# Local attention's scores three half tiles ahead of the turning, the first three behind the last feed-forward chunks

## The reference

```python
def _layer(x, wqkv, qs, ksc, wo, lg, lb, w1, b1, w2, b2):
    h = shift_token(x)
    q, k, v = jnp.split(h @ wqkv, 3, axis=-1)          # 8 heads of 64
    q = l2norm(q) * qs
    k = l2norm(k) * ksc
    q, k = rotary_xpos(q, k)
    o = local_attention(q, k, v)                       # window 128, looks one window back
    x = x + o @ wo
    h = layernorm(shift_token(x)) * lg + lb
    a, g = jnp.split(h @ w1 + b1, 2, axis=-1)          # hidden 682
    return x + (a * gelu(g)) @ w2 + b2
```

## Time and profile before

| what | value |
|---|---|
| median of 3 runs | 3101.23 us (3095.96 to 3109.24) |
| time of the profiled execution | 3108.76 us |
| its span | 3107.0 us |
| PE busy (matmul) | 2775.4 us, 89% of the span |
| DVE busy | 1622.3 us, 52% |
| ACT busy | 1200.9 us, 39% |
| POOL busy | 1076.6 us, 35% |

### The profile page before, as it was taken

One profiled execution on the slowest core, in us unless ns is written; L12 is line 12 of the kernel. 1 busy time (PEld: TensorE's weight loads), 2 busy tenths in 40 slices (PEclk: granted clock), 3 DMA queues, 4 the chain that ended last, 5 costly groups with the idle time before them and its releaser, 6 DMA issues. The chain is left out here.

```text
span 3107.0 us, 42331 instructions
## 1 busy us (share of the span) xinstructions
PE 2775.4 (89%) x15646; PEld 1867.6 (60%) x15646; DVE 1622.3 (52%) x3890; ACT 1200.9 (39%) x2254; POOL 1076.6 (35%) x769
## 2 busy tenths in 40 slices
PE   6999999999999999899989898999988579999990
PEld 3565656656565655645454545465544378999990
DVE  6656566565655555676767676767654310000002
ACT  4444453534444354444444444444442212222221
POOL 5423333342323333354535353535332201111112
PEclk9999999999999999999999999999987689999995
DMA  3000000000001011001010101010101179998875
GB/s 131 11 23 16 27 25 25 14 25 22 17 25 56 24 42 47 14 4 48 4 49 4 49 4 48 4 48 4 41 4 41 36 299 341 351 343 327 325 283 165
DMA packets 86054, 261.73 MB, mean 84 GB/s; under 512 B 10940, under 2 KB 50188, under 8 KB 67164
## 3 DMA queue, kind: packets, MB, share of 16 engines
q1 hardware_dynamic: 79372, 241.26, 21.4%
q0 software_dynamic: 6480, 17.77, 1.5%
HBM read 210.69 MB, written 44.12 MB: 82 GB/s over the span
## 5 line engine op out<-in xcount | busy, mean ns | idle before, releaser
L1176 POOL TENSOR_TENSOR s_qk<-s_qk,s_rrec 128x1024 f32<-128x1024 f32 (+1 forms) x128 | 215.7, 1685 | 578.4 <-DVE s_rrec L1330 578.2
L969 ACT ACTIVATE s_qk<-s_qk,s_mx 128x256 f32<-128x256 f32 (+1 forms) x512 | 239.9, 469 | 341.0 <-DVE s_mx L1324 340.3
L556 PE MATMUL s_pA<-s_w_wqkv,s_curT 128*128 128x512 f32 x768 | 354.7, 602 | 5.6 <-ACT s_curT L945 3.7
L1928 DVE COPY m_xT<-m_px 128x256 f32<-128x256 f32 x71 | 30.1, 425 | 475.5 <-PE m_px L1847 475.5
L1858 PEld LDWEIGHTS m_ph<-m_xT,m_w 128*128 128x128 f32 x2272 | 266.7, 193 | 5.4 <-issue 1.8
L1858 PE MATMUL m_ph<-m_xT,m_w 128*128 128x128 f32 x2272 | 267.3, 276 | 1.2 <-DVE m_xT L1928 1.2
L1872 PE MATMUL m_py<-m_w,m_hT 128*128 128x256 f32 x1136 | 256.8, 379 | 0.0
L556 PEld LDWEIGHTS s_pA<-s_w_wqkv,s_curT 128*128 128x128 f32 x768 | 142.6, 191 | 176.9 <-issue 163.4
L1419 DVE TENSOR_SCALAR s_pairs<-s_pD 128x1024 f32<-128x1024 f32 (+1 forms) x192 | 193.9, 1037 | 80.9 <-PE s_pD L699 79.3
L1792 POOL DMA_INDIRECT acc_s<-m_y,m_goal x71 | 68.1, 959 | 479.9 <-ACT m_y L1891 479.9
L1872 PEld LDWEIGHTS m_py<-m_w,m_hT 128*128 128x128 f32 x1136 | 210.4, 190 | 25.7
(11 more groups left out here) (224 smaller groups left out, 5172.5 us busy)
## 6 DMA issues: line engine op xcount, KB each, us to landing
m_w<-in_m_w SPq DMA_DIRECT2D x142, 1024.0 KB, 5.2
m_xin<-rows_s SPq DMA_DIRECT2D x71, 129.0 KB
m_acc<-acc_s SPq DMA_DIRECT2D x16, 512.0 KB, 5.2
s_cur<-in_x SPq DMA_DIRECT2D x8, 512.0 KB, 3.4
xn_s<-s_cur SPq DMA_DIRECT2D x8, 512.0 KB, 2.9
s_s_tm<-xn_s SPq DMA_DIRECT2D x8, 512.0 KB, 3.2
cur_s<-s_cur SPq DMA_DIRECT2D x8, 512.0 KB, 2.6
s_s<-s_s_tm SPq DMA_DIRECT2D x8, 512.0 KB, 2.6
```

Of the source, the lines that this page charges most:

```text
L556: last = nc.tensor.matmul(out, lhs(c), rhs(c), start=(c == 0), stop=(c == n - 1))
L969: last = nc.scalar.activation(pi, pi, ACT.Exp, scale=-1.0, bias=mx[:, u, i:i + 1], accum_out=rsum[:, u, i:i + 1])
L1176: nc.gpsimd.tensor_tensor(pi, pi, rrec[:, u, :].unsqueeze(2).broadcast_to((P, 4, 256 - lo)), ALU.mult).then_inc(p_rdy, 1)
```

## The change

`S` of half tiles 0, 1 and 2 moves from the u loop into the chunk loop, behind chunks 3, 4 and 5; `S` of half tile u + 1 then stands at u, from u = 2 on, behind `PT` of u - 2. DVE's `local_max`, ACT's `local_exp` and POOL's scaling move with it: `local_exp` of half tiles 0 and 1 stands behind the heads' copy of chunk 4 and behind the Gelu of chunk 5, that of half tile 2 at u = 1. In the u loop `PT` now stands ahead of `S` and of the latent scores' third round; on ACT `local_turned` stands ahead of `local_exp`. POOL scales half tiles 0 and 1 before and behind the second scatter of a latent stage.

```diff
             if s.ahead and c == 4:
                 j += [("qkT", k + 1, 3)]
+            if s.ahead and c >= NHC - 3:
+                j += [("S", k + 1, c - NHC + 3)]
         for u in range(2 * NT + 3):
-            if s.ahead and u < 2 * NT:
-                j += [("S", k + 1, u)]
             if s.ahead and 2 <= u < 2 * NT + 2:
                 j += [("PT", k + 1, u - 2)]
+            if s.ahead and 2 <= u < 2 * NT - 1:
+                j += [("S", k + 1, u + 1)]
...
                         heads_in(k + 1, 3)
+                    if s.ahead and c >= 4:
+                        local_exp(k + 1, c - 4)
                 for u in range(2 * NT + 3):
-                    if s.ahead and u < 2 * NT:
-                        local_exp(k + 1, u)
+                    if s.ahead and u == 1:
+                        local_exp(k + 1, 2)
                     if s.ahead and 2 <= u < 2 * NT + 2:
                         local_turned(k + 1, u - 2)
+                    if s.ahead and 2 <= u < 2 * NT - 1:
+                        local_exp(k + 1, u + 1)
...
+                if s.ahead:
+                    scale_probabilities(k + 1, 0)
+                if s.behind:
+                    scatter_rows(b - 1, 1)
+                if s.ahead:
+                    scale_probabilities(k + 1, 1)
...
                     if s.prep and c == 4:
                         again_apply(k + 1)
+                    if s.ahead and c >= NHC - 3:
+                        local_max(k + 1, c - NHC + 3)
+                    if s.ahead and c >= 4:
+                        local_reciprocal(k + 1, c - 4)
                     if s.behind and c == 5:
                         row_ends(b - 1, 1)
...
                 for u in range(2 * NT + 3):
-                    if s.ahead and u < 2 * NT:
-                        local_max(k + 1, u)
-                    if s.ahead and 1 <= u < 2 * NT + 1:
-                        local_reciprocal(k + 1, u - 1)
+                    if s.ahead and 2 <= u < 2 * NT:
+                        local_reciprocal(k + 1, u)
                     if s.lat and 6 < u < 11:
                         clipped(b, u - 7, (2,))
+                    if s.ahead and 2 <= u < 2 * NT - 1:
+                        local_max(k + 1, u + 1)
```

More of the change, by code:

```diff
@@ L870, in _ @@
                         head_transposes(k + 1, 3)
+                    if s.ahead and c >= NHC - 3:
+                        local_scores(k + 1, c - NHC + 3)
                 for u in range(2 * NT + 3):
-                    if s.ahead and u < 2 * NT:
-                        local_scores(k + 1, u)
+                    if s.ahead and 2 <= u < 2 * NT + 2:
+                        local_transposes(k + 1, u - 2)
                     if s.lat and 6 < u < 11:
                         latent_scores(b, u - 7, (2,))
-                    if s.ahead and 2 <= u < 2 * NT + 2:
-                        local_transposes(k + 1, u - 2)
+                    if s.ahead and 2 <= u < 2 * NT - 1:
+                        local_scores(k + 1, u + 1)
                     if s.ahead and u >= 3:
@@ L1226, in _ @@
                     scatter_rows(b - 1, 0)
-                    scatter_rows(b - 1, 1)
                 if s.prep:
                     reciprocal_roots(var_2, rstd_2, k + 1)
+                if s.ahead:
[4 more added lines that the diff above has]
+                    scale_probabilities(k + 1, 1)
                 if k == ITEMS - 1:
@@ L1235, in _ @@
                 for u in range(2 * NT + 3):
+                    if s.ahead and 2 <= u < 2 * NT:
+                        scale_probabilities(k + 1, u)
                     if s.ret and u in (4, 6, 8):
@@ L1243, in _ @@
                         query_sum(b, (u - 4) // 2)
-                    if s.ahead and u < 2 * NT:
-                        scale_probabilities(k + 1, u)
                     if s.lat and b == 0 and u == 2:
```

## The result

The changed kernel takes 3140.8 us (median of 4 runs) where the kernel before takes 3103.8 (median of 4): ratio 1.0124, 95% interval 1.0098 to 1.0151, 1.24% slower. That is above the range of 3090 to 3132. The profiled execution of the changed kernel takes 3139.22 us (span 3137.5), 30.5 more than the one of before; my sum had +6.

The account below looks back on a forecast made before the run. PE, busy 89% of the span, was taken as the bound. Retention -5.9, latent +10.2, stage -1 -5 and clock +7 gave +6 us, 3107 us on the median; range 3090 to 3132.

Parts of the forecast that it names:

- Chunk loop: Retention stages, up to w2: w2 starts 3.76 us later, 1.06 of it S2 done ahead, a loss of 2.70.
- the waits 0.73 and 0.72: Chunk loop, chunks 4 and 5: g waits for the banks of a heads' tile just turned, 0.73 and 0.72 us.
- w2's 1.77: End of the chunk loop: PE waits 1.77 us ahead of w2, behind the late Gelu and DVE's last fill.
- u loop of a retention stage: From w2 on: waits gone against new ones, stage end 627.6 instead of 628.14, -0.6 us a stage.
- The 2.83: Retention u loop: S4 waits 2.83 us in one piece for zaT's copy, which stands behind Exp 3 on ACT.
- Stage -1: Stage -1: no added load, the 3.20 ahead of S2 goes and five rounds gain 0.4 each, -5 us.
- Latent stages: Latent stages: w2 loses 2.2, net +1.4 us in six stages, +1.8 in stage 8, together +10.2.
- The clock: Whole program: waits of 2.83 and 4.0 bring more clock drops, 7 us taken, between nothing and 48.
- the second rival: Long waits bring the clock down in nearly every stage, 3 us for each of 14 stages: 3133 us, chance 0.2.
- the forecast: The prediction's own likeliest case, a near balance: +6 us, 3107 us on the median, chance 0.57.
- The tables: Chunk loop, before w2: a load is 1.28 us; two added loads cost 2.6 us and the Exp between 1.55.
- the third rival: A table switch costs about twice its load, w2 2.6 us later still in 15 stages: 3145 us, chance 0.03.

Follow-up runs that it names:

- exps_behind_gelu: The changed kernel with Exp of half tiles 0 and 1 behind the last Gelu on ScalarE, so no table loads are added: 3124.3 us, ratio 1.0061.
- scores_earlier: The changed kernel, early Exps behind the last Gelu, zaT and x1T emptied ahead of Exp, retention S0 and S1 behind chunks 1 and 2: 3061.8 us, 0.9865.
- stats_later: scores_earlier with the input statistics and norm of item k + 2 later on DVE in retention stages 0 to 5: 3064.3 us, ratio 0.9859.
- zat_first: The changed kernel with the emptying of zaT ahead of Exp 3 and of x1T ahead of Exp 5 on ScalarE: 3081.1 us, ratio 0.9925.
- first_three_only: The changed kernel with S of half tiles 0 to 2 still behind the chunks, but the u loop order of before: 3213.3 us, ratio 1.0334.
- the eight kernels named above: All kernels with the lead in the u loop and the statistics at u = 6; the product took 2.26 or 2.27 us in stages 0 to 5.

## Why the prediction was wrong

- **Chunk loop.** Right. Walked +3.76 to w2, measured +4.00; the waits 0.73 and 0.72 were 0.46 each, w2's 1.77 was 1.73. exps_behind_gelu and scores_earlier show both causes.
- **u loop of a retention stage.** This is the step that failed: "The sum: 580.77 + 42.8 + 2.83 + 1.2", -0.6 a stage. The 2.83 was there (2.69), but on the way from w2 to the next first product a clean stage takes 61.17, not 59.0. I had carried forward PE's work, the waits for ScalarE and one wait for DVE, and put the other waits for DVE at nothing. The clean stage of exps_behind_gelu has 5.9 us of waits (2.69, 0.78, 0.23, 1.08, 1.09) where I had 4.0. The 1.08 comes from a meeting that the lead brought about: DVE's product of the gated output runs beside POOL's scaling of a half tile and takes 1.58 longer. stats_later, where they don't meet, shows 1.16 of the 2.2. The 0.78 and the 0.23 (copies of outputs on DVE that TensorE now waits for; before, one such wait of 0.34) are read from the timeline only, and about 0.3 stay unassigned. A clean stage is 1.85 longer than before, seven of them 13 us, where I had -4.2.
- **Stage -1.** -5 was -0.5 (first product of stage 0 at 94.69, before 95.21). I left out that `zaT` is turned there too: S of half tile 4 waits 3.25 us. With the emptying first (zat_first), the first product of stage 0 comes at 92.58.
- **Latent stages.** Right in the sum: +1.4 a stage walked, and 72.66 + 85.35 - 156.83 = +1.2 without falls of the clock. The waits walked at 4.0, 0.73 and 1.02 are 3.5, 0.46 and 0.94. Inside the u loop it was in part luck: walked were 1.2 ahead of S4 and 2.0 ahead of S5, and stage 11 has 1.80 ahead of PT of half tile 1, none ahead of S4 and 1.50 ahead of S5.
- **The clock.** The term was +7 for the whole program. In stages 0 to 7 the falls cost 15.1 us in the changed kernel (each stage's length less the clean one, which for k = 6 is 0.7 more) and 5.6 in the kernel before: +9.5 there alone, and 13 - 0.4 (stage 7) + 9.5 is the 22.1 by which these stages are longer. So the mechanism of the second rival was at work, in seven retention stages of seven, but mostly at 1.5 us a fall, not 3. At the wait ahead of `lat` a fall begins in four of stages 9 to 14 (before: two). That rival's sum of 3133 still fell short, for its other terms were those of the forecast.
- **The tables.** 1.28 a load and no more, with 1.3 us a retention stage to be had back: the third rival is out. The figure of load and drain in the Trainium skill ("ScalarE: Activation LUTs", What ACT_TABLE_LOAD costs) agrees with these traces on the load (1.28) and not on the drain: the next ACTIVATE begins 0.01 us behind the load, and the load 0.02 or 0.03 behind the end of the instruction ahead of it, in either direction of the switch.

In sum, of the 24.3 us between my +6.2 and the 30.5, the walk of the retention stages is 18.5 and stage -1 is 4.5. The remaining 1 is the clock's excess less what the part behind stage 14 gives back (w2 of stage 15 is 34.1 later, the end 30.5). The length behind w2 of stage 15 varies by more than that between kernels (757 to 769), so this 1 says little. What I took for a balance was a loss of nearly 2 us a retention stage. The change as an idea wasn't bad: its two ends collide with the order of ScalarE's queue (Exp ahead of the last Gelu, Exp ahead of the emptying of `zaT` and `x1T`). With these turned round it gains 0.87%.

## What to carry to other kernels

When work is moved ahead on one engine, look on the emptying engine at what now stands behind it: the copy that frees banks for the next product goes ahead of the long Exp that nobody needs yet. Walk each engine's queue and not just the one that waits; an engine that was never late becomes so when the bound engine comes earlier. Look too at which pairs of DVE and POOL instructions now run side by side: here one such pair cost 1.58 us on DVE. A wait in one piece should be priced with the falls of the clock that it may bring, about one and a half microseconds for each stretch of 3.4 us here.

## What the runs showed of the hardware

A wait of the same 2.69 us at the same place was followed by 1.2 GHz in seven of seven retention stages of the changed kernel (stages of 140.2 us) and in every other one of exps_behind_gelu (stages of 137.4 us, 138.9 with a fall); one of 1.41 in two of seven of the kernel before, and in five of seven when another wait of 2.02 stood ahead of it. At `lat`, in stages 9 to 14, a fall begins in none of six with a wait of 0.73 (zat_first), in two with waits of 1.8 to 2.4 (before), in four with 3.4 to 3.5 (the changed kernel), and in all six with 2.81 (first_three_only). Its length alone doesn't decide. The length of the stage and the waits ahead of it differ between these kernels too, and I can't say from these runs which of them does. In the retention stages a stretch of 3.4 us costs 1.5 to 1.6 us in both kernels of the first pair, and the one of 6.8 us in before costs 4.0. So the falls have to be counted, stage by stage: the mean clock of stages 0 to 7 moves only from 1.00 to 0.98.

VectorE's TENSOR_TENSOR of 128x512 took 2.27 us in place of 0.69 where GpSimd's TENSOR_TENSOR of 128x1024 ran beside it, and that one took 2.28 in place of 1.89. It happened six times in each of the eight kernels named above, and never in the other five.
